# The second feed-forward weights of a graph kernel are split in 12 parts of 512 columns instead of 48 parts of 128

## The reference

```python
h = jnp.maximum(_layernorm(x, axis=-1), 0.0)
x = x + _L0_gnn_ref(h, adj, W_proj, W_att, b_att)     # 8 attention heads over each graph, relu
h = jnp.maximum(_layernorm(x, axis=-1), 0.0)
x = x + _L1_gnn_ref(h, adj, attn_w, ..., W1, b1, W2, b2, g1, beta1, g2, beta2)
```

```python
h = layernorm(x + agg, g1[l], beta1[l])
ff = gelu(h @ W1[l] + b1[l]) @ W2[l] + b2[l]           # W1 256x1024, W2 1024x256
x = layernorm(h + ff, g2[l], beta2[l])
```

## Time and profile before

| | |
|---|---|
| median of three runs | 1664.76 us |
| the profiled execution | 1663.78 us |
| its span | 1662.0 us |
| first part | 0 to about 345 us |
| its loop of 48 steps | about 100 to 315 us |
| second part | about 352 us to the end |

### The profile page before, as it was taken

One profiled execution on the slowest core, in us unless ns is written; L12 is line 12 of the kernel. 1 busy time (PEld: TensorE's weight loads), 2 busy tenths in 40 slices (PEclk: granted clock), 3 DMA queues, 4 the chain that ended last, 5 costly groups with the idle time before them and its releaser, 6 DMA issues. The chain is left out here.

```text
span 1662.0 us, 37278 instructions
## 1 busy us (share of the span) xinstructions
PE 1524.7 (92%) x11360; PEld 1282.6 (77%) x11360; DVE 1378.4 (83%) x4302; ACT 1087.1 (65%) x1946; POOL 891.4 (54%) x1008
## 2 busy tenths in 40 slices
PE   6888888827999999998999999899999999999995
PEld 6566666616888888887888888788888888888885
DVE  2889999967988989887888988888898888988852
ACT  1667777714677677665767666576777766677663
POOL 1667777723455355563545456444545656355464
PEclk9999999957999999999999999999999999999998
DMA  6233333250000011110001111100011211000001
GB/s 183 81 122 120 100 113 113 77 186 18 7 14 14 13 39 47 57 62 11 7 14 29 45 49 64 34 8 14 14 39 29 80 33 39 7 14 7 14 26 51
DMA packets 70894, 83.00 MB, mean 50 GB/s; under 512 B 29264, under 2 KB 54096, under 8 KB 70736
## 3 DMA queue, kind: packets, MB, share of 16 engines
q1 hardware_dynamic: 69104, 74.76, 15.2%
q0 software_dynamic: 816, 3.15, 0.6%
q10 hardware_dynamic: 816, 3.15, 0.5%
HBM read 38.95 MB, written 25.17 MB: 39 GB/s over the span
## 5 line engine op out<-in xcount | busy, mean ns | idle before, releaser
L805 ACT ACTIVATE bank<-bank,b_col 128x512 f32<-128x512 f32 x384 | 253.0, 659 | 365.2 <-PE bank L753 364.9
L765 PE MATMUL bank<-w_hi,hid_hi 128*128 128x256 f32 x1536 | 443.3, 289 | 17.8 <-DVE hid_lo L965 13.0
L765 PE MATMUL bank<-w_hi,hid_lo 128*128 128x256 f32 x1536 | 433.2, 282 | 0.0
L765 PE MATMUL bank<-w_lo,hid_hi 128*128 128x256 f32 x1536 | 432.8, 282 | 0.0
L965 DVE TENSOR_TENSOR hid_lo<-bank,hid_hi 128x512 fp32r<-128x512 f32 x384 | 259.1, 685 | 146.5 <-ACT hid_hi L810 143.0
L765 PEld LDWEIGHTS bank<-w_hi,hid_hi 128*128 128x128 f32 x1536 | 289.3, 188 | 53.8 <-DVE hid_lo L965 41.5
L753 PE MATMUL bank<-nT_hi,w_hi 128*128 128x512 f32 x768 | 318.2, 414 | 6.2 <-issue 4.8
L753 PE MATMUL bank<-nT_hi,w_lo 128*128 128x512 f32 x768 | 305.0, 397 | 4.8 <-issue 4.8
L753 PE MATMUL bank<-nT_lo,w_hi 128*128 128x512 f32 x768 | 304.0, 396 | 0.0
L765 PEld LDWEIGHTS bank<-w_lo,hid_hi 128*128 128x128 f32 x1536 | 289.6, 189 | 10.3
L765 PEld LDWEIGHTS bank<-w_hi,hid_lo 128*128 128x128 f32 x1536 | 289.4, 188 | 0.0
(11 more groups left out here) (122 smaller groups left out, 3076.9 us busy)
## 6 DMA issues: line engine op xcount, KB each, us to landing
x_other<-x_cur SPq DMA_DIRECT2D x96, 128.0 KB, 2.4
xin<-in_x_dram SPq DMA_DIRECT2D x16, 512.0 KB
first_block_out<-x_res SPq DMA_DIRECT2D x16, 512.0 KB
second_block_in<-x_act SPq DMA_DIRECT2D x16, 512.0 KB
x_cur<-second_block_in SPq DMA_DIRECT2D x16, 512.0 KB, 3.7
x_fin<-first_block_out SPq DMA_DIRECT2D x16, 512.0 KB, 3.6
out_dram<-x_fin SPq DMA_DIRECT2D x16, 512.0 KB, 2.9
xh_other<-xh SPq DMA_DIRECT2D x128, 33.0 KB, 1.9
```

Of the source, the lines that this page charges most:

```text
L765: mm = pe.matmul(FF[t // 2][:, (t % 2) * D:(t % 2 + 1) * D], a[:, r, t * P:(t + 1) * P], w[:, l, c, :], start=(c == 0 and t % 2 == 0 and p ...
L805: act.activation(h[:], h[:], ACT.Gelu, bias=b1_col[:, l, c:c + 1]).then_inc(s_gelu, 1)
```

## The change

The part that is split at a time grows from 128 to 512 columns, and it is split in step `t` = 0 of each round alone, so in 12 steps instead of 48. The waits and the counts follow.

```diff
-            W1P, W2P = KD * F // 4, L * CF * D // (NT - 16)
+            W1P, W2P = KD * F // 4, L * CF * D // (NT // 4 - 4)
...
-            def splits_w2(tau):
-                return not isinstance(tau, int)
+            def splits_w2(tau, t):
+                return not isinstance(tau, int) and t == 0
...
-                return raw[:].rearrange("p l f -> p (l f)").rearrange("p (n d) -> p n d", d=W2P)[:, tau - HEAD, :]
+                return raw[:].rearrange("p l f -> p (l f)").rearrange("p (n d) -> p n d", d=W2P)[:, tau // 4 - HEAD // 4, :]
...
-                    if splits_w2(tau):
+                    if splits_w2(tau, t):
                         act.copy(w2_part(w2_hi, tau), raw_part(tau)).then_inc(s_whi, 1)
...
-                    if splits_w2(tau):
-                        pool.wait_ge(s_whi, 4 * L + 1 + (tau - HEAD))
+                    if splits_w2(tau, t):
+                        pool.wait_ge(s_whi, 4 * L + 1 + (tau // 4 - HEAD // 4))
                         pool.tensor_tensor(w2_part(w2_lo, tau), raw_part(tau),
                                            w2_part(w2_hi, tau).bitcast(F32), ALU.subtract).then_inc(s_w2lo, 1)
```

More of the change, by code:

```diff
@@ L170, in graph_net @@
             FIRST_PART = 2
-            assert W2P * (NT - HEAD) == L * CF * D
+            assert W2P * (NT - HEAD) // 4 == L * CF * D
             def steps(eng, step):
@@ L187, in splits_w1 @@
                 return isinstance(tau, int) and FIRST_PART <= tau < FIRST_PART + 4 * L
-            def splits_w2(tau):
-                return not isinstance(tau, int)
+            def splits_w2(tau, t):
+                return not isinstance(tau, int) and t == 0
             def raw_part(tau):
-                return raw[:].rearrange("p l f -> p (l f)").rearrange("p (n d) -> p n d", d=W2P)[:, tau - HEAD, :]
+                return raw[:].rearrange("p l f -> p (l f)").rearrange("p (n d) -> p n d", d=W2P)[:, tau // 4 - HEAD // 4, :]
             def w2_part(w, tau):
-                return w.rearrange("p l c d -> p (l c d)").rearrange("p (n d) -> p n d", d=W2P)[:, tau - HEAD, :]
+                return w.rearrange("p l c d -> p (l c d)").rearrange("p (n d) -> p n d", d=W2P)[:, tau // 4 - HEAD // 4, :]
             def counted(S):
@@ L456, in _ @@
                 steps(pool, step)
-                pool.wait_ge(s_w2lo, NT - HEAD)
+                pool.wait_ge(s_w2lo, NT // 4 - HEAD // 4)
                 pool.wait_ge(s_rows, 16 * 3)
```

## The result

The changed kernel took 1687.83, 1682.27 and 1689.28 us; the median on record is 1688.55 of four runs. A fourth run of 4023.05 us counts in that median and in no comparison. The kernel before took 1664.38 beside it. Ratio 1.0135, interval 1.0116 to 1.0154; forecast were 1671.4 us (1667.4 to 1674.6), a ratio of 1.004. The direction is right, the size isn't. The profiled execution took 1687.83 us with a span of 1686.0, 24.0 more than before.

A forecast was written before the change was run, and what follows sets the result against it. A circle of waits through DVE, POOL and ACT was taken to bound the loop at 17.96 us a round. The new round of 18.54 (9.52 + 9.02) gave +6.6 us on 1664.76, so 1671.4 us, range 1667.4 to 1674.6.

The forecast's parts named there:

- The circle: Loop: DVE's headout frees POOL to nmr, ACT to scored, leaky two steps later; halves 8.70 and 9.26 us.
- Term 1: Loop, steps 1 to 3 lose w_lo; only the stall of shifted in step 2 counts: -0.24 us a round.
- Term 2: Step 0: 512-column w_lo on POOL holds DVE off 1.16 us, delaying shifted and headout by 0.82; first half 9.52.
- The low bound: Step 0 w_lo: hold grows from 0.34 by only 0.21 per 128 columns, to 0.96 us; delay 0.62.
- Term 3: Step 0 w_hi on ACT, 512 columns once: hT 0.32 us later, covered by the delay of shifted; costs nothing.
- Term 4: Step 0: w_lo's lead of 0.34 us over shifted stays, as step 3 to step 0 remains 4.73.
- Sum: Loop: new round 18.54 us, +0.58; 11 rounds +6.4, first round +0.2, together +6.6 us.
- A: Loop: POOL's full length counts and vare also loses in step 0; 0.835 a round, 9.4 us, 1674.2; chance 8%.
- B: Loop: wide w_lo comes after shifted has started, x_res held back about 0.5; +0.27 a round, 1668.0 us; chance 4%.
- C: Loop: long instruction doesn't hold the ports through; only the stall of step 2 goes, -2.9 us, 1661.9; chance 10%.
- D: Loop: steps are paced by the amount of work on ACT, so faster: -5.9 us, 1658.9; chance 4%.

The follow-up runs named there:

- the large filler: Changed kernel plus two products of constants (256 and 128 columns) on TensorE in the gap at t=2: 1667.66 us, ratio 1.0023.
- the small one: Changed kernel plus one product of constants (128 columns) on TensorE in the gap at t=2: 1674.96 us, ratio 1.0062.
- the filler at t=0: Changed kernel plus two products of constants (256 and 128 columns) on TensorE at t=0 instead of t=2: 1668.73 us, ratio 1.0028.
- the pieces: Changed kernel with the 512-column w_lo as four instructions of 128 columns in a row, all at t=0: 1667.06 us, ratio 1.0021.

## Why the prediction was right in sign and wrong in size

- **The circle** as the bound, its two halves of 8.70 and 9.26: borne out as far as the clock stays up. With the large filler the halves are 9.93 and 8.91 in the mean of rounds 2 to 12, against 9.52 and 9.02 foretold.
- **Term 1** (-0.24 for the stall of t=2): `shifted` takes 0.67 at t=1 to 3 as said. How much time that gave back by itself isn't shown; the kernel before gained nothing from it.
- **Term 2** (a hold of 1.16, a delay of 0.82): `w_lo` 1.27 and a delay of 0.85 with a lead of 0.30. Taking the price from a collision of the same size was right. By the full length of the instruction, as the Trainium skill (SBUF — State Buffer, "SBUF: two separate sides") words it, it would be 1.27 less the lead of 0.30, 0.97; the trace is 0.12 below that again. But "nothing is added there" behind `headout` was wrong: `nmr` of t=1 runs into `shifted` of t=1 (0.45 for 0.20). In the kernel before, `nmr` came 0.15 ahead of `shifted` (213.69, 213.84). The prediction's own numbers turn that order round: `nmr` hangs on `headout` and moves by 0.82 to 214.51, while `leaky` of t=1 moves only to 212.31 and `shifted`, 1.93 behind it, to 214.24. I had looked for collisions of `w_lo` only. The low bound rests on a hold that grows by 0.21 us per 128 columns; no row shows that figure. The rows of the two sizes give 0.28 ((1.295 - 0.46) / 3), and the hold grew from 0.34 to 1.15, by 0.27.
- **Term 3** (`w_hi` free): right, 0.61 long, with `hT` 0.51 behind its start as estimated, and the kernel with only that edit takes the same time.
- **Term 4** (the lead stays 0.34): wrong. It was 0.29 or 0.30 in six rounds and 0.10 to 0.15 in four; with the large filler it was 0.10 in six and 0.15 in one, and `shifted` then took up to 1.73, a delay of 1.05.
- **Sum**: +0.58 a round foretold. Without clock falls it is 10.1 / 12 = 0.84 with the large filler, 9.71 / 12 = 0.81 with the small one, about +10 us in the loop. The surplus over 0.58 is the second collision (0.25) and the shorter lead, less a second half that is 0.11 shorter than foretold.
- **The failed step** is the one on what bounds the loop: "at a granted TensorE clock of 0.99, so practically at 2.4 GHz", which I then carried over to the new kernel. No rival spoke of it. I followed the delay from POOL to ACT and back to DVE and left out that TensorE is fed by the same ACT; what the delay does to the clock stood at nothing, without a reason. The eight long rounds took 164.8 instead of 143.7 us, +21.1, of which 8 x 0.84 = 6.7 are the ports' and about 14 the clock's (read directly, t=2 to t=3 is 1.67 longer in each of the eight, 13.4). With the four short rounds (+2.9) that is the +24.0 of the loop: the missing 17 us are some 14 of clock, the rest the second collision and the lead. That the clock is behind them is shown by the 0.25 us product in the gap, after which no round is long.
- A smaller step that failed is "nothing is added there" in term 2, with the second collision in its place.
- **Rivals** A to D all fell. A had the nearest number, by another mechanism; B, in the kernel with `w_lo` behind `shifted`, came out at 1679 and not 1668 us: `neg` and `nmr` of t=1 (0.44) collide, and four rounds lose the clock.

What stays open: why rounds with the same idle stretches keep the clock in one place and lose it in another (11 of 50, in the changed kernel itself, with the filler at t=0 and with `w_lo` behind `shifted`), whether the stretch ahead of the transpose is a cause or only goes along, and why the second part has one fall less in two kernels whose second part is unchanged. None of the versions was faster than the kernel before.

## What to carry to other kernels

A long GpSimd instruction next to VectorE work with two SBUF inputs is priced by its lead and its length, and the sum is then walked once more through every engine of the circle, with the order of each near-simultaneous pair checked again. If a delay leaves TensorE idle for a large part of a microsecond in a loop that otherwise keeps it busy, the clock belongs among the rivals; a gap of that size is no proof, for the pieces had it without a fall. A product of constants in the gap tells whether it is the clock, if the rounds of the loop are read and not the total. Work that runs beside the bounding engine was cheaper in small instructions here: four pieces in a row cost half of one wide instruction in the loop (+4.9 against +10.1 us), and 48 pieces spread over the steps cost least.

## What was not expected of the hardware

- TensorE's granted clock fell to half for about 3 us and came back, 8 and 11 times in a loop of 12 rounds, behind idle stretches of 0.3, 0.9 and 0.2 us; a 0.25 us product in the middle one stopped it (8 and 11 long rounds, then none). With the 0.9 alone, and 0.16 or less ahead of it, none of 41 rounds lost the clock.
- A two-column GpSimd instruction waits for the ports like a wide one: `nmr` 0.45 for 0.20. A two-column VectorE instruction waited for 0.9 us (`neg` 1.03 for 0.17).
- In one part of a program the same instructions took 1339.1 or 1345 to 1348 us, by one clock fall more or less around 1080 us.
